# A graph layer's edge stage: the second layer two groups behind the first, and eight buffers for gathered rows

## The chip, the cores and the metric

The kernel runs on one core of one Trainium2 chip. The metric is the device time of an execution in microseconds. TensorE is called PE here, VectorE DVE, ScalarE ACT, GpSimd POOL and SyncE SP.

## What is computed

Two layers of a graph network over 6250 nodes with 128 features and 100,000 edges, each with a residual and a normalisation. The first is attention over edges. The change is in the second, of which this is the core:

```
x = _layernorm(x + attention(x, ...))
row, col = src, dst
edge_in = concatenate([x[row], x[col], edge_features])
h = silu(edge_in @ eW1 + eb1)
edge_feat = silu(h @ eW2 + eb2)
agg = segment_sum(edge_feat, row, num_segments=6250)
out = silu(concatenate([x, agg]) @ nW1 + nb1) @ nW2 + nb2
x = _layernorm(x + out)
```

## The kernel before

The edges are sorted by source into 832 tiles of 128 edges, so that each tile's sources lie in one window of 128 nodes. The kernel has the stages count, place, score, softmax, weigh, middle, edges, node layers and normalisation, one after the other. The edge stage (`edges`, from L1670) takes the tiles in 208 groups of four, G = 4. All of a group's steps have their own function, and each engine runs its own loop over the groups (`each_group`): `step(g, r)` calls the works of that engine, each for the group at some distance `by` from g. The distances and the order of that list are the schedule; engines meet by semaphores alone. Some groups at both ends are written out, the rest is a hardware loop over RING = 4 groups.

Per group:

- SP loads rows of lane numbers for two groups at once, 256 KB (L1712), into one of two buffers.
- DVE `index` (L1733) turns the destinations into int32 for the gather. `front` makes the one-hot matrices of the sources (`ed_oht`, L1738) and copies the attributes (`ed_attrs`, L1742). `by_edges` makes one-hots the other way (`ed_ohf`, L1748). `back` adds the four sums to the table `vals` (L1758).
- POOL `gather` (L1724) issues four indirect DMAs, one a tile, each fetching 128 rows of 512 bytes by destination into `ed_bg`, a ring of four buffers. Before a gather it waits until the inputs of the group four earlier are done (`s_z`).
- PE `turn` (L1819) transposes the attributes into the one PSUM tile `ps_ed_oht`; `inputs` (L1829, L1831, L1834) makes a tile's first layer in `ps_z` (two PSUM banks): attributes, three bf16 parts of the source's row by one-hot, and the gathered row, transposed; `second` (L1842, L1845) is the second layer in `ps_ed_o` (two banks); `sums` (L1855) sums the features by source in `ps_ed_s` (two banks).
- ACT `turned` (L1791) copies the transposed attributes to SBUF (`ed_attr_t`, two buffers), `hidden` (L1796) makes `ed_hts` = silu of the first layer (two buffers), `feature` (L1801) makes `ed_efs` = silu of the second.

In an execution of `step(g)` PE does the transpose of g+1, the inputs of g, the sums of g-2 and the second layer of g-1, in that order. The sums of g-2 need ACT's `ed_efs` of g-2, whose second layer is the last thing of PE's step before. ACT does turned g+1, hidden g, feature g-1; DVE index g+3, front g+2, by_edges g, back g-3.

Of the kernel before, what the change touches and what calls it, by code (L numbers as in the profile page):

```python
# [651 lines left out]
RING = 4  # L652


def each_group(eng, step, lead=0, lag=0, groups=NG, rings=1):


    for g in range(-lead, rings * RING):
        step(g, g % RING)
    with eng.Fori(rings, groups // RING - 1) as i:  # L660
        for r in range(RING):
            step(RING * i + r, r)
    for g in range(groups - RING, groups + lag):
        step(g, g % RING)


def group_at(g, r, by, groups=NG):

    there = not isinstance(g, int) or 0 <= g + by < groups
    return g + by, (r + by) % RING, there  # L670


def ring_count(g, r, each):

    return (g - r + RING) * (each // RING)
# [993 lines left out]
def edges(c, a):  # L1669
# [7 lines left out]
    s_b = semaphores(nc, c.stack, "ed_b_in0 ed_b_in1 ed_b_in2 ed_b_in3")  # L1677
# [3 lines left out]
    with ExitStack() as t:  # L1681
# [4 lines left out]
        w2 = sb("w_2", [P, F], F32)  # L1686
# [4 lines left out]
        ohf = sb("ed_ohf", [P, RING, G, P], F32)  # L1691
# [11 lines left out]
        with nc.Block() as block:  # L1703
            @block.sync
            def _(sp):
                sp.dma_start(w2[:, :], a["eW2"]).then_inc(s_w, 16)
                sp.dma_start(b2[:, :], row_vector(a["eb2"], F)).then_inc(s_w, 16)

                def lanes(g, r):
                    if r % 2 == 0:  # L1710
                        wait_count(sp, s_oht, g - 2)
                        sp.dma_start(lane_rows[:, r // 2, :], lanes_of(c, g * G, 2 * G)).then_inc(s_lr[r // 2], 16)  # L1712
                each_group(sp, lanes, rings=2)

            @block.gpsimd
            def _(pool):
                pool.memset(attr[:, :, :], 0.0).then_inc(s_pad, 1)

                def gather(g, r):
                    pool.wait_ge(s_idx, g + 1)  # L1720
                    wait_count(pool, s_z, g - RING + 1)
                    pool.sem_inc(s_turn, 1)
                    for k in range(G):
                        pool.indirect_dma_start(bg[:, r, k * F:(k + 1) * F], None, c.b_dram[:, :],  # L1724
                                                bass.IndirectOffsetOnAxis(ap=idx[:, r, k:k + 1], axis=0)
                                                ).then_inc(s_b[r], 16)
                each_group(pool, gather)

            @block.vector
            def _(dve):  # L1730
                def index(g, r):
                    wait_count(dve, s_b[r], (g - r) * (16 * G // RING))
                    dve.tensor_copy(idx[:, r, :], c.rec[:, bass.ds(g * G, G), C_DST]).then_inc(s_idx, 1)  # L1733

                def front(g, r):
                    dve.wait_ge(s_lr[r // 2], ring_count(g, r, 16))
                    wait_count(dve, s_z, g - RING + 1)
                    dve.tensor_scalar(oht[:, r].rearrange("p k n -> p (k n)"),  # L1738
                                      lane_rows[:, r // 2, r % 2 * GP:(r % 2 + 1) * GP], c.pid[:, 0:1], None,
                                      ALU.is_equal).then_inc(s_oht, 1)  # L1740
                    wait_count(dve, s_tr, g - RING + 1)
                    dve.tensor_copy(attr[:, r, 0:K].rearrange("p (j x) -> p j x", j=3),  # L1742
# [3 lines left out]
                def by_edges(g, r):  # L1746
                    wait_count(dve, s_sum, g - RING + 1)
                    dve.tensor_tensor(ohf[:, r], c.iota[:, :].unsqueeze(1).to_broadcast([P, G, P]),  # L1748
# [11 lines left out]
                def step(g, r):  # L1760
                    for by, work in ((3, index), (2, front), (0, by_edges), (-3, back)):
                        at, slot, there = group_at(g, r, by)
# [21 lines left out]
                each_group(dve, step, lead=3, lag=3, rings=2)  # L1784

            @block.scalar
            def _(act):
                def turned(g, r):
                    act.wait_ge(s_tr, g + 1)
                    wait_count(act, s_z, g - 1)  # L1790
                    act.activation(att[:, r % 2, :], pst[:, 0:P], ACT.Copy).then_inc(s_att, 1)  # L1791

                def hidden(g, r):
                    act.wait_ge(s_z, g + 1)
                    wait_count(act, s_o, g - 1)
                    act.activation(ht[:, r % 2, :], psz[r % 2][:, :], ACT.Silu).then_inc(s_h, 1)  # L1796
# [7 lines left out]
                def step(g, r):  # L1804
                    for by, work in ((1, turned), (0, hidden), (-1, feature)):
                        at, slot, there = group_at(g, r, by)
                        if there:
                            work(at, slot)
                each_group(act, step, lead=1, lag=1, rings=2)

            @block.tensor
            def _(pe):
# [3 lines left out]
                def turn(g, r):  # L1816
                    pe.wait_ge(s_at, g + 1)
                    wait_count(pe, s_att, g)
                    pe.transpose(pst[:, 0:P], attr[:, r, :], c.identb[:, :]).then_inc(s_tr, 1)  # L1819

                def inputs(g, r):
# [5 lines left out]
                    for k in range(G):  # L1827
                        z = psz[b][:, k * P:(k + 1) * P]
                        pe.matmul(z, wc[:, k, :], att[:, b, :], start=True, stop=False)  # L1829
                        for j in range(3):  # L1830
                            pe.matmul(z, c.tab[:, j, bass.ds(win[k] * F, F)], oht[:, r, k, :], start=False, stop=False)  # L1831
                        if k == 0:
                            pe.wait_ge(s_b[r], ring_count(g, r, 16 * G))
# [4 lines left out]
                def second(g, r):  # L1838
# [5 lines left out]
                    for k in range(G):  # L1844
                        ins = pe.matmul(pso[b][:, k * F:(k + 1) * F], ht[:, b, k * P:(k + 1) * P], w2[:, :],  # L1845
# [3 lines left out]
                def sums(g, r):  # L1849
# [4 lines left out]
                    for k in range(G):  # L1854
                        ins = pe.matmul(pss[b][:, k * P:(k + 1) * P], ef[:, b, k, :], ohf[:, r, k, :],  # L1855
# [3 lines left out]
                def step(g, r):  # L1859
                    for by, work in ((1, turn), (0, inputs), (-2, sums), (-1, second)):  # L1860
                        at, slot, there = group_at(g, r, by)
# [172 lines left out]
```

## Time and profile before

| | us |
|---|---|
| median of 3 runs | 6032.9 |
| runs | 6025.1 to 6042.95 |
| profiled execution | 6037.5 |
| its span | 6035.8 |
| edge stage in it | 4577.6 to 5943.5 |
| POOL busy in the span | 3887.0 (64%) |
| PE busy in the span | 2949.4 (49%) |

The profile is of one execution; its own time stands 4.6 us over the median. Times in it count from the span's start. "Idle before" in a row is the time for which that engine did nothing before it, and the name behind it is what ended it: "issue" is nothing that the profile shows, "remote" a semaphore whose sender it can't name. The end of a matmul is modelled, its start is recorded. A name such as `ps_z<-ident,ed_bg` reads output, arrow, inputs; buffer numbers are left out.

### The profile page before, as it was taken

How to read it: one execution, taken by the hardware profiler on the slowest of the kernel's cores; microseconds unless marked ns; L12 is line 12 of the kernel's file. 1: busy time of each engine (PE TensorE's matmuls, PEld its weight loads, DVE VectorE, ACT ScalarE, POOL GpSimd, SP SyncE). 2: the span in 40 equal slices, each digit the busy share in tenths (PEclk: the TensorE clock that was granted, in tenths of full speed). 3: DMA queues.
4: the chain of work that ended last, by engine and by line, in shares of the span. 5: the costliest groups of instructions: out<-in, count | busy, mean ns of one | idle time of the engine just before them, and what ended most of it. 6: DMA issues, size and time to landing. Idle time of an engine off the chain costs nothing. (4 is left out here: it accounts for less than half of the span.)

```text
span 6035.8 us, 82769 instructions
## 1 busy us (share of the span) xinstructions
PE 2949.4 (49%) x21843; PEld 2592.4 (43%) x21844; DVE 2376.2 (39%) x6253; ACT 765.7 (13%) x1646; POOL 3887.0 (64%) x4130
## 2 busy tenths in 40 slices
PE   6444443442222222212666666566474666666666
PEld 4333332331222222212555555555454565565554
DVE  6554555552222222348333333333253333333334
ACT  0111110110000000001111111111121221122112
POOL 0677887885666666641888888888814555555551
PEclk9765565665566666556777788877766888888888
DMA  2200000002222222210443434343351222222222
GB/s 90 87 10 10 11 11 11 11 11 90 66 66 66 67 65 64 67 41 8 35 36 35 36 35 36 35 36 35 35 145 53 59 61 60 62 60 60 60 60 60
DMA packets 299979, 293.29 MB, mean 49 GB/s; under 512 B 61763, under 2 KB 239104, under 8 KB 298911
## 3 DMA queue, kind: packets, MB, share of 16 engines
q0 software_dynamic: 200128, 176.61, 18.5%
q1 hardware_dynamic: 96926, 103.02, 6.0%
q10 hardware_dynamic: 2880, 13.11, 0.5%
q8 instruction: 21, 0.34, 0.0%
q14 instruction: 24, 0.20, 0.0%
HBM read 198.61 MB, written 93.92 MB: 48 GB/s over the span
## 5 line engine op out<-in xcount | busy, mean ns | idle before, releaser
L1080 POOL DMA_INDIRECT sums_dram<-we_merged_rows,we_idx x832 | 1286.2, 1546 | 420.4 <-issue 206.7
L1724 POOL DMA_INDIRECT ed_bg<-b_rows_dram,ed_idx x832 | 796.4, 957 | 563.1 <-issue 284.9
L787 POOL DMA_INDIRECT sc_k<-k_rows_dram,sc_idx x832 | 797.0, 958 | 441.3 <-issue 253.8
L642 POOL DMA_INDIRECT records_dram<-rec_out,row_idx x784 | 783.0, 999 | 207.3 <-issue 111.0
L873 PE MATMUL ps_q<-tab,sc_oht 128*128 x1664 | 307.6, 360 | 825.9 <-DVE sc_oht L802 414.2
L873 PEld LDWEIGHTS ps_q<-tab,sc_oht 128*128 128x128 f32 x1664 | 288.1, 269 | 842.0 <-issue 842.0
L1231 PE MATMUL ps_merged<-we_rows,we_same_dst 128*128 128x129 f32 x1664 | 332.0, 361 | 586.5 <-issue 438.0
L1758 DVE TENSOR_TENSOR vals<-vals,ps_ed_s 128x128 f32 x832 | 239.0, 287 | 848.4 <-PE ps_ed_s L1855 403.8
L1231 PEld LDWEIGHTS ps_merged<-we_rows,we_same_dst 128*128 128x128 f32 x1664 | 283.4, 257 | 622.2 <-issue 612.8
L817 DVE TENSOR_TENSOR sc_prods<-ps_q,sc_k 128x1024 f32<-128x1024 f32 x104 | 127.2, 1223 | 821.8 <-remote 756.5
L1855 PE MATMUL ps_ed_s<-ed_ohf,ed_efs 128*128 128x128 f32 x1664 | 281.1, 322 | 337.3 <-ACT ed_efs L1801 291.7
L1133 DVE SCALAR_TENSOR_TENSOR we_firsts<-we_merged_rows,lane_unmark,two_marks 128x4 f32<-128x4 f32 x208 | 46.3, 222 | 1013.5 <-ACT we_merged_rows L1176 1013.5
L1855 PEld LDWEIGHTS ps_ed_s<-ed_ohf,ed_efs 128*128 128x128 f32 x1664 | 247.1, 228 | 362.3 <-issue 337.6
L593 PE MATMUL ps_table<-place_ohw,place_oh 128*128 128x400 bf16 (+7 forms) x784 | 160.9, 381 | 450.0 <-DVE place_ohw L216 337.0
L1831 PE MATMUL ps_z<-ed_oht,tab 128*128 128x128 bf16 x2496 | 309.1, 228 | 63.1 <-issue 62.3
L593 PEld LDWEIGHTS ps_table<-place_ohw,place_oh 128*128 128x128 bf16 x784 | 111.3, 162 | 508.9 <-issue 452.3
L1211 PE MATMUL ps_dst_row<-ident,we_dsts 128*128 128x128 f32 x1664 | 329.7, 366 | 0.0
L1211 PEld LDWEIGHTS ps_dst_row<-ident,we_dsts 128*128 128x128 f32 x1664 | 314.6, 281 | 0.0
L629 POOL COPY rec_out<-records 128x16 f32 (+1 forms) x784 | 190.7, 252 | 183.2 <-POOLq L276 112.1
L1176 ACT ACTIVATE we_merged_rows<-ps_merged 128x516 f32<-128x516 f32 x208 | 124.8, 600 | 1280.0 <-DMA sums_dram<-we_merged_rows,we_idx 1265.9
L1221 PE MATMUL ps_v<-value_tab,we_oht 128*128 x1664 | 276.0, 318 | 0.1
L1845 PEld LDWEIGHTS ps_ed_o<-w,ed_hts 128*128 128x128 f32 x1664 | 262.2, 224 | 18.4 <-issue 4.3
(291 smaller groups left out, 6230.3 us busy)
## 6 DMA issues: line engine op xcount, KB each, us to landing
sc_lane_rows<-lanes_dram SPq DMA_DIRECT2D x104, 256.0 KB
ed_lane_rows<-lanes_dram SPq DMA_DIRECT2D x104, 256.0 KB
sc_k<-k_rows_dram,sc_idx POOLq DMA_INDIRECT x832
sums_dram<-we_merged_rows,we_idx POOLq DMA_INDIRECT x832
ed_bg<-b_rows_dram,ed_idx POOLq DMA_INDIRECT x832
sums_dram<-zero_rows ACTq DMA_DIRECT2D x20, 640.0 KB, 10.2
records_dram<-rec_out,row_idx POOLq DMA_INDIRECT x784
mi_rows<-sums_dram SPq DMA_DIRECT2D x48, 256.0 KB, 4.4
```

The lines of the kernel that those rows point to most:

```text
L593: ins = pe.matmul(table[:, k:PG, :], ohl[:, b, :, k], ohw[:, b, k, :].unsqueeze(1).to_broadcast([P, PG - k, WC]), start=(k == 0), stop=Tru ...
L642: pool.indirect_dma_start(c.rec_rows, bass.IndirectOffsetOnAxis(ap=idx[:, b, j:j + 1], axis=0), out[:, b, j, :], None, bounds_check=SLOTS ...
L787: pool.indirect_dma_start(kg[:, r, k * F:(k + 1) * F], None, c.k_dram[:, :], bass.IndirectOffsetOnAxis(ap=idx[:, r, k:k + 1], axis=0)).the ...
L873: ins = pe.matmul(psq[b][:, k * F:(k + 1) * F], oht[:, b, k, :], c.qtab[:, bass.ds(win[k] * F, F)], start=True, stop=True)
L1080: pool.indirect_dma_start(c.acc_dram[k][:, :], bass.IndirectOffsetOnAxis(ap=idx[:, r, k:k + 1], axis=0), rows[:, r, k, 0:F], None, compute ...
L1211: ins = pe.matmul(psd[:, k * P:(k + 1) * P], dst[:, r, k:k + 1].to_broadcast([P, P]), c.ident[:, :], start=True, stop=True)
L1221: ins = pe.matmul(psv[b][:, k * F:(k + 1) * F], oht[:, b, k, :], c.vtab[:, bass.ds(win[k] * F, F)], start=True, stop=True)
L1231: ins = pe.matmul(merged[b][:, k, 0:F + 1], same[:, b, k, :], con[:, b, k, :], start=True, stop=True)
L1724: pool.indirect_dma_start(bg[:, r, k * F:(k + 1) * F], None, c.b_dram[:, :], bass.IndirectOffsetOnAxis(ap=idx[:, r, k:k + 1], axis=0)).the ...
L1831: pe.matmul(z, c.tab[:, j, bass.ds(win[k] * F, F)], oht[:, r, k, :], start=False, stop=False)
L1845: ins = pe.matmul(pso[b][:, k * F:(k + 1) * F], ht[:, b, k * P:(k + 1) * P], w2[:, :], start=False, stop=(k == G - 1))
L1855: ins = pe.matmul(pss[b][:, k * P:(k + 1) * P], ef[:, b, k, :], ohf[:, r, k, :], start=True, stop=True)
```

## The change

All of it is in the edge stage. Its loops run over eight groups instead of four, on all engines. Distances change as in the table.

| engine | before | after |
|---|---|---|
| PE | turn +1, inputs 0, sums -2, second -1 | turn +2, inputs 0, second -2, sums -3 |
| ACT | turned +1, hidden 0, feature -1 | turned +2, hidden 0, feature -2 |
| DVE | index +3, front +2, by_edges 0, back -3 | index +7, front +3, by_edges -1, back -4 |

`ed_bg` and `ed_idx` have eight buffers instead of four, `ed_attr_t` and `ed_hts` four instead of two. PSUM stays as it was. To make room, `ed_ohf`, `ed_efs` and the weights `w_2` move into free columns of the table `work`, and carry that name in the rows of order below.

```
@@ edges, buffers
+        w2 = c.work[:, NP - F:NP]
+        spare = lambda n, m: c.work[:, NT * 3 + n * GP:NT * 3 + m * GP].rearrange("p (b k n) -> p b k n", b=m - n, k=G)
+        ohf = spare(0, RING)
-        att = sb("ed_attr_t", [P, 2, P], BF16)
-        idx = sb("ed_idx", [P, RING, G], I32)
-        bg = sb("ed_bg", [P, RING, G * F], F32)
+        att = sb("ed_attr_t", [P, RING, P], BF16)
+        idx = sb("ed_idx", [P, ER, G], I32)
+        bg = sb("ed_bg", [P, ER, G * F], F32)
-        ht = sb("ed_hts", [P, 2, GP], F32)
-        ef = sb("ed_efs", [P, 2, G, F], F32)
+        ht = sb("ed_hts", [P, RING, GP], F32)
+        ef = spare(RING, RING + 2)
@@ gpsimd, gather
-                    wait_count(pool, s_z, g - RING + 1)
+                    wait_count(pool, s_z, g - ER + 1)
@@ scalar
-                    wait_count(act, s_z, g - 1)
+                    wait_count(act, s_z, g - RING + 1)
...
-                    wait_count(act, s_o, g - 1)
+                    wait_count(act, s_o, g - RING + 1)
@@ tensor, step
-                    for by, work in ((1, turn), (0, inputs), (-2, sums), (-1, second)):
-                        at, slot, there = group_at(g, r, by)
+                    for by, work in ((2, turn), (0, inputs), (-2, second), (-3, sums)):
+                        at, slot, there = group_at(g, r, by, NG, ER)
...
-                each_group(pe, step, lead=1, lag=2, rings=2)
+                each_group(pe, step, lead=2, lag=3, ring=ER)
```

On PE, inside the loop, this stands in a row before, from the last matmul of a group's inputs to the first of the next (ISA and REGISTER_ALU are register work of the sequencer):

```order
L1834 MATMUL ps_z1<-ident,ed_bg 128x128
L88 ISA
L1855 MATMUL ps_ed_s1<-ed_ohf,ed_efs 128x128 x4
L1842 MATMUL ps_ed_o0<-b_2_rows,ones 128x512
L1845 MATMUL ps_ed_o0<-w_2,ed_hts 128x128 x4
L1819 MATMUL ps_ed_oht<-identb,ed_attrs 128x128
```

And at the same place after:

```order
L1837 MATMUL ps_z1<-ident,ed_bg 128x128
L1845 MATMUL ps_ed_o1<-b_2_rows,ones 128x512
L1848 MATMUL ps_ed_o1<-work,ed_hts 128x128 x4
L88 ISA
L1858 MATMUL ps_ed_s0<-work 128x128 x4
L1820 REGISTER_ALU
L1822 MATMUL ps_ed_oht<-identb,ed_attrs 128x128
```

The second layer has moved ahead of the sums and is of the group two back, the sums of the group three back.

On DVE, at the opening of the stage, before:

```order
L1782 SCALAR_TENSOR_TENSOR b_2_rows<-b_2_parts,ident,b_2_rows 128x128 x2
L1733 CAST ed_idx<-records 128x4 x2
L1738 TENSOR_SCALAR ed_oht<-ed_lane_rows,partition_number 128x512
L1742 COPY ed_attrs<-work 128x72
L1733 CAST ed_idx<-records 128x4
```

And after:

```order
L1785 SCALAR_TENSOR_TENSOR b_2_rows<-b_2_parts,ident,b_2_rows 128x128 x2
L1736 CAST ed_idx<-records 128x4 x5
L1741 TENSOR_SCALAR ed_oht<-ed_lane_rows,partition_number 128x512
L1745 COPY ed_attrs<-work 128x72
L1736 CAST ed_idx<-records 128x4
```

Five groups of gather indices stand ahead of the first one-hot instead of two.

## Rows read from the trace of the kernel before

**Rows 1.** Busy time by stretch: the score stage, the edge stage.
```profile
core 0: us, PE busy (x) PEld busy (x) DVE busy (x) ACT busy (x) POOL busy (x), PEclk, DMA share, GB/s
1428.00:2672.00 1244.00, 329.32 (x1768) 301.55 (x1768) 357.39 (x622) 35.52 (x154) 797.01 (x832) 0.61 0.26 66
4577.60:5943.50 1365.90, 901.64 (x7904) 819.75 (x7903) 477.24 (x1658) 272.87 (x625) 796.41 (x832) 0.82 0.24 60
```

**Rows 2.** Group of the gathers: busy, mean ns, idle before and what ended it.
```profile
L1724 POOL DMA_INDIRECT ed_bg<-b_rows_dram,ed_idx x832 | 796.4, 957 | 563.1 <-issue 284.9 <-remote 165.5 <-PE ps_z L1834 88.8
```

**Rows 3.** Timeline, the edge stage's end: start, us, instruction, idle before.
```profile
5926.79 0.94 POOL L1724 DMA_INDIRECT ed_bg<-b_rows_dram,ed_idx  x1 [0.30 <-issue]
...
5932.84 1.05 PE L1845 MATMUL ps_ed_o<-w,ed_hts 128*128 128x128 f32 x8
...
5936.20 1.05 PE L1845 MATMUL ps_ed_o<-w,ed_hts 128*128 128x128 f32 x8
```

**Rows 4.** Waits of the edge stage: total us, times, longest us.
```profile
ACT ed_efs L1801 <- remote: 496.9, 53, 10.7
...
PE ps_ed_s L1855 <- ACT ed_efs L1801: 291.7, 56, 8.3
...
PE ps_z L1834 <- DMA ed_bg<-b_rows_dram,ed_idx: 6.7, 2, 4.6
```

**Rows 5.** Timeline of one cycle of four groups in the edge stage.
```profile
5035.04 0.60 ACT L1796 ACTIVATE ed_hts<-ps_z 128x512 f32<-128x512 f32 x1 [4.85 <-remote]
...
5035.78 0.94 POOL L1724 DMA_INDIRECT ed_bg<-b_rows_dram,ed_idx  x1 [1.83 <-issue]
...
5037.47 1.05 PE L1845 MATMUL ps_ed_o<-w,ed_hts 128*128 128x128 f32 x8
...
5039.66 0.28 PE L1834 MATMUL ps_z<-ident,ed_bg 128*128 128x128 f32 x1
...
5044.52 0.94 POOL L1724 DMA_INDIRECT ed_bg<-b_rows_dram,ed_idx  x1 [0.30 <-issue]
5047.35 0.60 ACT L1801 ACTIVATE ed_efs<-ps_ed_o 128x512 f32<-128x512 f32 x1 [10.56 <-remote]
...
5048.08 2.07 PE L1855 MATMUL ps_ed_s<-ed_ohf,ed_efs 128*128 128x128 f32 x8 [8.14 <-ACT ed_efs L1801]
5048.25 0.94 POOL L1724 DMA_INDIRECT ed_bg<-b_rows_dram,ed_idx  x1 [2.79 <-remote]
...
5049.94 0.63 PE L1842 MATMUL ps_ed_o<-b_rows,ones 128*128 128x512 bf16 x1
...
5050.37 1.92 PE L1845 MATMUL ps_ed_o<-w,ed_hts 128*128 128x128 f32 x8
...
5054.93 0.94 POOL L1724 DMA_INDIRECT ed_bg<-b_rows_dram,ed_idx  x1 [1.99 <-PE ps_z L1834]
```

**Rows 6.** Busy time by stretch: that cycle, and after its late signal.
```profile
5026.00:5052.00 26.00, 16.48 (x152) 15.23 (x150) 9.43 (x35) 5.13 (x12) 15.20 (x17) 0.81 0.23 61
...
5047.50:5054.00 6.50, 5.92 (x41) 5.68 (x42) 2.21 (x8) 1.87 (x5) 3.78 (x4) 0.61 0.16 44
```

**Rows 7.** Timeline of the edge stage's opening.
```profile
4591.02 0.42 PE L1834 MATMUL ps_z<-ident,ed_bg 128*128 128x128 f32 x1
...
4601.44 0.94 POOL L1724 DMA_INDIRECT ed_bg<-b_rows_dram,ed_idx  x1 [0.30 <-issue]
...
4606.03 0.60 ACT L1796 ACTIVATE ed_hts<-ps_z 128x512 f32<-128x512 f32 x1 [12.49 <-remote]
```

**Rows 8.** DMA queues of 4700 to 5900: packets, MB, share of 16 engines.
```profile
q0 software_dynamic: 23522, 48.22, 16.1%
q1 hardware_dynamic: 13251, 24.13, 7.8%
```

**Rows 9.** Waits of the score stage.
```profile
DVE sc_prods L817 <- remote: 756.5, 47, 28.7
```

More of the change, by code:

```diff
@@ L652, with each_group, group_at, ring_count @@
 RING = 4
[L655 to L667, printed above, removed]
+SR = 8
+ER = 8
+def each_group(eng, step, lead=0, lag=0, groups=NG, rings=1, ring=RING):
+    for g in range(-lead, rings * ring):
+        step(g, g % ring)
+    with eng.Fori(rings, groups // ring - 1) as i:
+        for r in range(ring):
+            step(ring * i + r, r)
+    for g in range(groups - ring, groups + lag):
+        step(g, g % ring)
+def group_at(g, r, by, groups=NG, ring=RING):
     there = not isinstance(g, int) or 0 <= g + by < groups
-    return g + by, (r + by) % RING, there
-def ring_count(g, r, each):
-    return (g - r + RING) * (each // RING)
+    return g + by, (r + by) % ring, there
+def ring_count(g, r, each, ring=RING):
+    return (g - r + ring) * each // ring
 def load_windows(eng, c, regs, side, g, n=1):
@@ L1676, in edges @@
     s_lr = semaphores(nc, c.sems, "ed_lanes_in0 ed_lanes_in1")
-    s_b = semaphores(nc, c.stack, "ed_b_in0 ed_b_in1 ed_b_in2 ed_b_in3")
+    s_b = semaphores(nc, c.stack, " ".join(f"ed_b_in{n}" for n in range(ER)))
     (s_turn,) = semaphores(nc, c.sems, "ed_gather_turn")
@@ L1726, in gather @@
                                                 ).then_inc(s_b[r], 16)
-                each_group(pool, gather)
+                each_group(pool, gather, ring=ER)
             @block.vector
@@ L1760, in step @@
                 def step(g, r):
-                    for by, work in ((3, index), (2, front), (0, by_edges), (-3, back)):
-                        at, slot, there = group_at(g, r, by)
+                    for by, work in ((7, index), (3, front), (-1, by_edges), (-4, back)):
+                        at, slot, there = group_at(g, r, by, NG, ER)
                         if there:
@@ L1783, in _ @@
                                              in1=b2k[:, :], op0=ALU.mult, op1=ALU.add).then_inc(s_bias, 1)
-                each_group(dve, step, lead=3, lag=3, rings=2)
+                each_group(dve, step, lead=7, lag=4, ring=ER)
             @block.scalar
@@ L1804, in step @@
                 def step(g, r):
-                    for by, work in ((1, turned), (0, hidden), (-1, feature)):
-                        at, slot, there = group_at(g, r, by)
+                    for by, work in ((2, turned), (0, hidden), (-2, feature)):
+                        at, slot, there = group_at(g, r, by, NG, ER)
                         if there:
                             work(at, slot)
-                each_group(act, step, lead=1, lag=1, rings=2)
+                each_group(act, step, lead=2, lag=2, ring=ER)
             @block.tensor
```

36 lines of the change are left out of this document (17 added, 19 removed).

## The prediction, made before the changed kernel ran

> **What bounds the kernel now.** The change touches only the edge stage, so I first cut the trace into stages: 1365.9 of the 6035.8 us are the edge stage, from the first gather to the last addition [rows 1]. There PE is busy for 902 us, POOL for 796 us, DVE and ACT far less. No engine fills the stage; it is bound by a chain. A gather instruction takes 957 ns on average [rows 2] with 0.30 us to the next [rows 3], 1.25 us in all, and there are 832: POOL alone would need 832 × 1.25 = 1040 us. PE alone, at the end of the stage where nothing stops it, starts the second layer of one group at 5932.84 and of the next at 5936.20 [rows 3], 3.4 us a group, 707 us for 208 groups. The stage runs at 1350 us from the first gather at 4577.6 to the end of the last at 5927.7 [rows 3], 6.49 us a group.
>
> The waits of the stage say who stands still [rows 2, 4]: PE before the sums for 291.7 us, all on the activation of the features (L1801); ACT before that activation for 496.9 us, on something the profile can't name ("remote"); POOL for 165.5 and 88.8 us on freed gather buffers. PE waits on landed gathers (L1834) for 6.7 us in all. So gathered rows are always there in time, and POOL's pauses come from PE.
>
> The timeline of one cycle shows what "remote" is [rows 5]. PE's last matmul of a second layer starts in the row at 5037.47 and that row ends at 5038.5; the next inputs end at 5039.9. ACT, idle for 10.56 us, starts the features only at 5047.35. Its one unmet condition is that second layer: the end of a matmul is known to the others 8.8 us after the record says it was over. POOL, too, waits for the end of the inputs recorded at 5039.9 and resumes at 5048.25. PE has meanwhile reached the sums and stands for 8.14 us. I call this a late signal. The late signals come out together about 2 us after POOL has run out of gathers (its last one before ends at 5045.5). Such a cycle takes 26.0 us and four groups [rows 6]; a weaker one is at its start, where ACT gets an ended input layer after 4.85 us idle, at 5035.04 [rows 5].
>
> The Trainium skill ("Perfetto Trace Analysis", the section on per-engine timelines) says that the end shown for TensorE is estimated and that the semaphore follows once PSUM has acknowledged the writes. This trace agrees that the two can differ, here by 8.8 us; the page gives no reason for such a size, and nothing below uses it.
>
> **The change part by part.** No matmul, activation, addition or transfer is added or removed; 832 gathers and 104 loads of lane rows stay.
>
> *Order on PE.* Before: transpose, inputs of g, sums of g-2, second layer of g-1. After: transpose of g+2, inputs of g, second layer of g-2, sums of g-3. Between the end of a second layer and the sums that need it there was one input layer, after it an input layer, another second layer and the transpose. With prompt signals neither order holds PE up: the groups of [rows 3] follow each other at 3.4 us. Under a late signal PE now gets further. At 5039.9 it has the inputs done and stands at the sums, which are 2.07 us when done at 5048.08 and are followed by a second layer of 0.63 + 1.92 us, at a granted clock of 0.61 [rows 5, 6], the lower level (1.2 GHz) for most of it. These 4.2 us stand between the release at 5047.3 and the next input layer. In the new order they depend on older signals and would lie before the stop; after the release PE goes straight to the input layer. That layer's end permits POOL's next gather. It came at about 5054, and POOL paused 1.99 us before 5054.93 [rows 5]; 4.2 us earlier is 49.8, before POOL is through with the gathers it has (5053.0). The pause shrinks to the usual 0.30: 1.69 us a cycle. I take exactly this, because POOL at 1.25 us a gather then is the later of the two. The other two pauses of the cycle, 2.79 and 1.83 us [rows 5], stay: they end with a late signal, which the order doesn't touch. 1350 us / 26.0 = 52 cycles, 52 × 1.69 = **-88 us**. Bounds: zero, if PE stops at another step just as early; and 52 × (1.69 + 2.49 + 1.53) = -297 us if all three pauses go.
>
> *What could stop PE instead.* The transposed attributes have one PSUM tile, so the transpose of g+3 waits for ACT's copy of g+2, whose transpose is one step old. That is one whole step (3.4 us) against the 1.5 us of an input layer before. PE therefore still stops inside every late signal, one step later at most: this is why I don't take more than one pause.
>
> *ACT and DVE.* ACT's order stays turn, hidden, feature with the feature two behind; nothing is queued behind a new wait that was not there. DVE's one-hots (L1738) for g+3 now wait for the inputs of g-1 instead of g-2 before g+2; behind that wait stand the additions of g-4, and PE's transpose waits for DVE. DVE needs 0.35 + 0.18 us to produce them; a whole PE step lies between. Zero while that holds; if a late signal catches it, PE stops where it would have stopped anyway.
>
> *Eight buffers of gathered rows.* In the cycle they hide nothing, since PE waits for landed rows for 6.7 us in the whole stage [rows 4]. They change the ends of the stage. At the opening, POOL ran five groups without a stop, until the gather of 4601.44; ACT's signal from PE's second input layer, recorded as over by 4591.4, came at 4606.03 [rows 7]. With eight buffers POOL may run nine groups. If signals come only when it stops, that is 4 × 5.0 = **+20 us**; the lower bound is zero. At the close POOL is up to four more groups ahead, and those run at 3.4 instead of 6.49 us: 4 × 3.1 = **-12 us**.
>
> *Loops of eight groups.* Half as many branches, twice the code. In the steady part of the stage there are no instruction transfers: the queues between 4700 and 5900 are two, both of data [rows 8]. The Trainium skill ("Runtime: NRT & Kernel Launch", instruction fetch mechanics) warns that a taken branch to code outside the resident pages forces a fetch. This trace shows no such fetch for a loop of four groups, and can't show one for eight. I take zero. As a bound from rows: 24 returns of the loop, each at worst a pause like the 2.79 us one, is +67 us.
>
> **Sum.** -88 + 20 - 12 = -80 us on the profiled execution's 6037.5 us, 5957.5. That execution is 4.6 us over the median of the runs; against the median, 6032.9 - 80 = **5953 us**.
>
> **The rivals.**
> *Nothing to gain (chance 0.17).* The late signals set the pace alone, whatever the order. For: ACT's 496.9 us of "remote" are longer than PE's 291.7. Against: the 4.2 us of work that stood after the release. Then the opening's +20 and the close's -12 remain, 6041 us.
>
> *The deep ring frees POOL (0.16).* In the score stage the ring holds 32 tiles too (4 buffers of 8), and its 832 gathers took 1244 us with the same late signals (DVE waits for "remote" 756.5 us there) [rows 1, 9]. At that pace the edge stage's 1366 us shrink by 122, 5911 us. If the late signals lost their grip entirely, the stage would be POOL's 1040 us and some 16 us of close, 310 less, 5723 us; I give this end 0.07 of the 0.16.
>
> *The deep ring feeds the late signals (0.21).* They come out when POOL stops. With room for eight groups POOL can run longer before it stops, and PE stands meanwhile, as at the opening, where a signal was 14.6 us late during a run of five groups. Where a cycle's longest run grows by one group it costs 5.0 us. Against: in a steady state POOL can only refill what PE has freed, two groups a run, whatever the depth. It decides from the point where PE, running at 3.4 us against POOL's 5.0, leaves POOL a backlog of more than two groups when a late signal begins. At one group more in every second cycle, with no pause saved: 26 × 5.0 = +130, 6163 us; in every cycle 6293 us.
>
> *The change doesn't do what it says.* The order on PE shows that it does; no chance of its own.
>
> **How the numbers follow.** One pause of three saved has 0.46, the largest share: 5953 us, in itself 5925 to 6000. With 0.16 for the deep ring, 0.17 for nothing and 0.21 for longer late signals the shares are complete. What a measurement of this kernel can tell from no change is about 0.3%, 18 us. Faster by more than that: 0.46 + 0.16 = 0.62; within it 0.17; slower 0.21. The range for 8 in 10 goes down to 5850 (two pauses of three gone, 52 × (1.69 + 1.53) = 167 us, and some), leaving out the 0.07 of a freed POOL, and up to 6080, leaving out some 0.12 of longer late signals.
>
> **What would show it.** In the profile after: PE's wait before the sums (291.7 us) nearly gone, with one before the transpose or the inputs in its place that is smaller; POOL's idle time before the gathers (563.1 us, of which 250 are the 0.30s) down to about 480; a cycle of about 24.3 us for four groups. The edge stage at 1286 us. ACT still waits for "remote" in pieces of 5 to 9 us. If these pieces are 14 us and more, and POOL runs more than two groups between pauses, the third rival is right. If PE's idle time merely moves and POOL's pauses stay three a cycle, the first is. Instruction transfers between 4700 and 5900 would mean that the longer loop costs. The forecast is wrong in its root if late signals have nothing to do with POOL's stops, since then the eight buffers and the saved pause are priced on the wrong row.

## The result and the profile after

The changed kernel takes 6069.2 us (median of 6, 6061.0 to 6102.0), the kernel before on the same chip 6028.7 us (median of 6). The ratio is 1.0072, with a 95% interval of 1.0058 to 1.0086: slower, where the forecast was 5953 us. The profiled execution took 6066.8 us.

Everything ahead of the edge stage is 7 us shorter (it starts at 4571.0 instead of 4577.6), and what stands behind it is as long as before. The edge stage goes from 1366 to 1402.7 us. Its row, from the first gather to the last addition (columns as in [rows 1]):

```profile
4571.00:5973.70 1402.70, 1035.33 (x7904) 902.31 (x7903) 482.55 (x1656) 286.90 (x625) 831.51 (x832) 0.79 0.24 58
```

The gathers' group (busy, mean ns, idle before and what ended it; [rows 2] is its answer before) and DVE's additions, from the profile after:

```profile
L1727 POOL DMA_INDIRECT ed_bg<-b_rows_dram,ed_idx x832 | 831.5, 999 | 550.0 <-issue 238.7 <-DVE ed_idx L1736 190.3 <-remote 110.8
L1761 DVE TENSOR_TENSOR vals<-vals,ps_ed_s 128x128 f32 x832 | 238.9, 287 | 581.2 <-remote 439.7
```

The additions in the kernel before, in the grouping of its edge stage:

```profile
L1758 DVE TENSOR_TENSOR vals<-vals,ps_ed_s 128x128 f32 x832 | 239.0, 287 | 848.4 <-PE ps_ed_s L1855 403.8 <-remote 341.5 <-issue 13.6
```

Before, POOL waited for the index like this (total us, times, longest):

```profile
POOL ed_bg L1724 <- DVE ed_idx L1733: 23.8, 23, 9.4
```

And waits after ([rows 4] before):

```profile
POOL ed_bg L1727 <- DVE ed_idx L1736: 190.3, 69, 9.4
DVE ed_oht L1741 <- remote: 292.3, 76, 36.8
ACT ed_hts L1799 <- remote: 403.0, 78, 35.5
ACT work L1804 <- remote: 277.6, 60, 8.7
DVE vals L1761 <- remote: 439.7, 85, 10.4
PE ps_ed_s L1858 <- issue: 103.7, 167, 1.2
```

Two things are new. PE's 291.7 us before the sums are gone, as forecast: no row for ACT stands there now, but "issue" pieces of 103.7 us do. And POOL, which waited for freed buffers, now waits for DVE's conversion of the indices (`ed_idx`), 190.3 us in 69 waits. The 69 are not alike: one of 9.4 us is the stage's first gather, which waits as long in the kernel before; 27 are the 0.30 us that stand between any two gathers; the other 41 take 4.2 us on average, 173 us in all. One such place in the timeline after (start, us, instruction, idle before):

```profile
5009.60 1.06 PE L1858 MATMUL ps_ed_s<-work 128*128 128x128 f32 x8
...
5015.20 0.95 POOL L1727 DMA_INDIRECT ed_bg<-b_rows_dram,ed_idx  x1 [0.30 <-issue]
...
5018.08 1.57 DVE L1761 TENSOR_TENSOR vals<-vals,ps_ed_s 128x128 f32 x4 [7.75 <-remote]
...
5018.10 0.60 ACT L1799 ACTIVATE ed_hts<-ps_z 128x512 f32<-128x512 f32 x1
...
5019.57 0.16 DVE L1736 CAST ed_idx<-records 128x4 int32 x1
...
5020.60 1.01 POOL L1727 DMA_INDIRECT ed_bg<-b_rows_dram,ed_idx  x1 [4.45 <-DVE ed_idx L1736]
```

Late signals arrive together at 5018.1: ACT gets its input layer, and DVE the sums, whose row on PE starts at 5009.60 and ends 7.4 us before. POOL ran out at 5016.15. But DVE's next work is the additions for g-4 (1.57 us), and only behind them stands the index for g+7. POOL resumes at 5020.60, 2.5 us later than the signal and 0.87 us after the index is made. In [rows 5] it resumed 0.90 us after ACT on a late signal; so some 1.6 of the 2.5 us are DVE's.

It is the additions that hold the index up. Ahead of each of the 41 waits, DVE's last long wait was the one before the additions, on "remote", and not the one before the one-hots. In the kernel before, in the cycle of [rows 5], the additions had started on time, and the index was made 7.5 us ahead of the late signal:

```profile
5038.17 1.58 DVE L1758 TENSOR_TENSOR vals<-vals,ps_ed_s 128x128 f32 x4
5039.67 0.16 DVE L1733 CAST ed_idx<-records 128x4 int32 x1
```

There PE stood in front of the next sums, and those of the older group had been signalled: 403.8 us of DVE's wait before the additions end directly on PE's sums, 341.5 us on "remote". Now PE goes on through second layer and sums, and a larger part of the sums' signals is late: 439.7 of 581.2 us are on "remote". This reading of the two rows of additions fits the places looked at; what the place of the index is worth is tested below.

### The profile page after: what moved, and what is told of

It is laid out like the page before. It is cut to its first block and busy times, and to the rows that moved or that the text cites. A ratio compares the mean times of both kernels' runs of the same rounds, so it can differ in the third digit from the quotient of the medians.

```text
span 6065.1 us, 82347 instructions
## 1 busy us (share of the span) xinstructions
PE 3093.8 (51%) x21843; PEld 2678.6 (44%) x21844; DVE 2383.3 (39%) x6253; ACT 780.3 (13%) x1646; POOL 3927.4 (65%) x4130
## 5 line engine op out<-in xcount | busy, mean ns | idle before, releaser
L1082 POOL DMA_INDIRECT sums_dram<-we_merged_rows,we_idx x832 | 1287.0, 1547 | 420.5 <-issue 208.9
L1727 POOL DMA_INDIRECT ed_bg<-b_rows_dram,ed_idx x832 | 831.5, 999 | 550.0 <-issue 238.7
L875 PE MATMUL ps_q<-tab,sc_oht 128*128 x1664 | 311.8, 364 | 796.4 <-DVE sc_oht L804 436.6
L1761 DVE TENSOR_TENSOR vals<-vals,ps_ed_s 128x128 f32 x832 | 238.9, 287 | 581.2 <-remote 439.7
L1834 PE MATMUL ps_z<-ed_oht,tab 128*128 128x128 bf16 x2496 | 349.8, 253 | 96.2 <-issue 95.3
L1858 PE MATMUL ps_ed_s<-work 128*128 128x128 f32 x1664 | 300.4, 316 | 104.8 <-issue 103.7
L1848 PE MATMUL ps_ed_o<-work,ed_hts 128*128 128x128 f32 x1664 | 302.1, 323 | 62.2 <-issue 59.0
L1848 PEld LDWEIGHTS ps_ed_o<-work,ed_hts 128*128 128x128 f32 x1664 | 284.9, 235 | 106.1 <-issue 92.0
L1858 PEld LDWEIGHTS ps_ed_s<-work 128*128 128x128 f32 x1664 | 260.9, 227 | 117.8 <-issue 116.7
L1837 PE MATMUL ps_z<-ident,ed_bg 128*128 128x128 f32 x832 | 276.6, 332 | 35.8 <-issue 30.2
```

Of the source, the lines that this page charges most:

```text
L875: ins = pe.matmul(psq[b][:, k * F:(k + 1) * F], oht[:, b, k, :], c.qtab[:, bass.ds(win[k] * F, F)], start=True, stop=True)
L1082: pool.indirect_dma_start(c.acc_dram[k][:, :], bass.IndirectOffsetOnAxis(ap=idx[:, r, k:k + 1], axis=0), rows[:, r, k, 0:F], None, compute ...
L1834: pe.matmul(z, c.tab[:, j, bass.ds(win[k] * F, F)], oht[:, r % RING, k, :], start=False, stop=False)
L1837: ins = pe.matmul(z, bg[:, r, k * F:(k + 1) * F], c.ident[:, :], start=False, stop=True, is_transpose=True)
L1848: ins = pe.matmul(pso[b][:, k * F:(k + 1) * F], ht[:, r % RING, k * P:(k + 1) * P], w2[:, :], start=False, stop=(k == G - 1))
```

## Experiments

A ratio is always to the kernel before, run in between on the same chip. The kernel before took 6029, 5964 and 5965 us on three chips, and 5516, 5521 and 5521 us on three others. What that is comes under "the chip"; until then all runs are on the slower three, but for the paced ones. Where two kernels ran on different chips, compare their ratios and not their times.

### The two halves apart

`order_alone` has four buffers and loops of four in the changed kernel:

```
-ER = 8
+ER = 4
...
-                    for by, work in ((7, index), (3, front), (-1, by_edges), (-4, back)):
+                    for by, work in ((3, index), (3, front), (-1, by_edges), (-4, back)):
```

> The new order (second layer two groups behind, sums three, additions four, one-hots three ahead) with four buffers of gathered rows and loops of four groups, so without the other half of the change. Theory 1, the index queued behind the one-hots: in the profile after the change POOL waits 69 times, 190.3 us in all, 2.76 us each, for DVE's index, because DVE now stands before the one-hots of g+3 until the inputs of g-1 are known to be done, and behind that wait stand 0.5 us of one-hots, 0.7 us of the one-hot by edges and 1.6 us of additions before the next index. This order has the same slack of one group, so by theory 1 it is as slow as the whole change, 6060 to 6080 us, with POOL waiting for ed_idx again. Theory 2, the deep ring feeds the late signals: the order alone keeps its gain, 5950 us. Theory 3, the loop of eight groups costs: about 6030 us, as before.

Measured: 6072.9 us, ratio 1.0063 (1.0044 to 1.0081). Here, too, POOL waits for the index in 50 places inside the stage, each behind DVE's wait before the additions. The group of gathers in its profile:

```profile
L1727 POOL DMA_INDIRECT ed_bg<-b_rows_dram,ed_idx x832 | 822.6, 989 | 584.5 <-issue 244.2 <-DVE ed_idx L1736 234.8 <-remote 93.3
```

`ring_alone` keeps the eight buffers and puts back all of the old order:

```
-                    for by, work in ((7, index), (3, front), (-1, by_edges), (-4, back)):
+                    for by, work in ((7, index), (2, front), (0, by_edges), (-3, back)):
...
-                    for by, work in ((2, turn), (0, inputs), (-2, second), (-3, sums)):
+                    for by, work in ((1, turn), (0, inputs), (-2, sums), (-1, second)):
```

> The old order with eight buffers of gathered rows, index seven ahead and loops of eight groups. Theory 1 (index queued): the one-hots are two ahead and the index stays two groups ahead of what POOL needs, so POOL does not wait for it; 6030 us, perhaps some 20 more for a longer opening. Theory 2 (deep ring feeds the late signals): slower by the third rival's price, 6100 us or more, with POOL running more than two groups between pauses. Theory 3 (long loop): 6060 us or more, PE's idle pieces called issue at the place where the loop returns.

Measured: 6034.6 us, ratio 1.0010 (1.0000 to 1.0020).

```profile
L1727 POOL DMA_INDIRECT ed_bg<-b_rows_dram,ed_idx x832 | 803.7, 966 | 540.5 <-issue 244.0 <-remote 192.6 <-PE ps_z L1837 80.2
```

The loss is the order's, and the wait for the index comes with the order. Eight buffers, an index seven ahead and loops of eight together cost 6 us (12 at the interval's upper end). The third rival's price (130 us) and that of a longer loop fall.

### The index out of the way

`index_early` is the changed kernel with one line of DVE's order changed (and the lead from 7 to 8):

```
-                    for by, work in ((7, index), (3, front), (-1, by_edges), (-4, back)):
+                    for by, work in ((3, front), (8, index), (-1, by_edges), (-4, back)):
```

> The changed kernel with DVE's index for g+8 right behind the one-hots for g+3, ahead of the one-hot by edges and the additions, instead of the index for g+7 behind all of them. Nothing else moves. Theory 1: POOL's 190.3 us of waiting for the index go, 69 x 2.76; what of it the freed buffers or late signals do not take back is the gain, 5960 to 6010 us. Theory 2 and theory 3: unchanged, 6069 us, with POOL waiting for PE or for remote events where it waited for the index.

`ahead_four` gives the index a lead of four more groups in another way, by holding POOL back:

```
-                    wait_count(pool, s_z, g - ER + 1)
+                    wait_count(pool, s_z, g - RING + 1)
```

> The changed kernel, in which POOL may gather only four groups ahead instead of eight (it waits for the inputs of g-4 instead of g-8); buffers, order, index and loops of eight are those of the change. Theory 1: the index is now made seven ahead and needed three ahead, so POOL never waits for it; 5960 to 6000 us. Theory 2: as fast as the order alone, 5950 us. Theory 3: no better than the change, 6070 us. Theories 1 and 2 are told apart by the order alone.

Measured: `index_early` 6013.0 us, 0.9972 (0.9962 to 0.9983); `ahead_four` 6005.6 us, 0.9959 (0.9947 to 0.9971), each some 3 to 6 us above what theory 1 allowed. The gathers of `index_early`, then of `ahead_four`:

```profile
L1727 POOL DMA_INDIRECT ed_bg<-b_rows_dram,ed_idx x832 | 844.4, 1015 | 476.7 <-issue 252.7 <-remote 202.2 <-PE ps_z L1837 12.4
```

```profile
L1727 POOL DMA_INDIRECT ed_bg<-b_rows_dram,ed_idx x832 | 843.7, 1014 | 481.0 <-issue 379.9 <-remote 77.5 <-DVE ed_idx L1736 15.8
```

The place of one 0.16-us instruction in DVE's queue is worth 56 us: more than the whole loss. With it out of the way the change is faster than the kernel before, by 16 us (by 23 where POOL stays four ahead). In `index_early` the one-hots for g+3, with their new wait, still stand in front of the index; only the one-hot by edges and the additions have gone behind it. So it was these that cost, not the one-hots' wait.

`order_early_third` needs nothing of the eight buffers: `order_alone` with the index for g+4 behind the one-hots for g+3.

```
-                    for by, work in ((3, index), (3, front), (-1, by_edges), (-4, back)):
+                    for by, work in ((3, front), (4, index), (-1, by_edges), (-4, back)):
```

> order_index_early, unchanged, on another chip. Where signals are late (before 5960 us or more), theory 1, that the index in DVE's queue was the order's whole loss: ratio 0.995 to 0.998. Theory 2, that the eight buffers or the loops of eight are needed: 1.000 to 1.006. Where they are prompt (before some 5520 us): 0.998 a third time.

Measured: 5941.9 us against 5964.7, ratio 0.9959 (0.9945 to 0.9972). Theory 1 holds: the index was the order's whole loss, and eight buffers and longer loops are not needed. This and `ahead_four` are the best versions found.

```profile
L1727 POOL DMA_INDIRECT ed_bg<-b_rows_dram,ed_idx x832 | 838.1, 1007 | 474.2 <-issue 253.8 <-remote 203.3 <-DVE ed_idx L1736 9.4
```

### Where the rest of the expected 88 us is

POOL's idle time falls in `ahead_four` from 563.1 [rows 2] to 481.0 us, 82 less, almost the 88 forecast. But the gathers themselves are busy for 843.7 instead of 796.4 us, 47 more, and the close grows by 4: -82 + 47 + 4 = -31 us, the measured change of the stage (1366.2 to 1335.2). The longer gathers are these, in the profile of the change:

```profile
5044.19 0.68 DVE L1751 TENSOR_TENSOR work<-iota,lanes 128x512 f32<-128x512 f32 x1
...
5044.23 1.47 POOL L1727 DMA_INDIRECT ed_bg<-b_rows_dram,ed_idx  x1 [0.30 <-issue]
...
5046.00 0.95 POOL L1727 DMA_INDIRECT ed_bg<-b_rows_dram,ed_idx  x1 [0.30 <-issue]
```

A gather that starts while the by-edges one-hot runs takes until some 0.8 us after the one-hot's end. Over the trace, the 75 gathers that start within 0.3 us behind a one-hot's start take 1.25 to 1.46 us (means of each tenth); those that start ahead of it take about 0.95. All 132 gathers over 1.1 us overlap this one-hot (23 in the kernel before). The additions, which read PSUM, lengthen none by themselves (203 gathers overlap them alone, 0.957 us at most). The Trainium skill ("GPSIMD Engine Reference", key points) says that GpSimd shares its SBUF interfaces with VectorE, with contention from VectorE instructions that have two SBUF inputs; this instruction has two, and the traces agree. With the new order far more gathers meet a one-hot (166 of over 1.1 us in `ahead_four`); probably because one signal now releases DVE and POOL together.

To see what that costs, three kernels hold the one-hot's row of numbers (`iota`) in a spare bank of PSUM (`psi`), on top of `ahead_four`, of the kernel before, and of `index_early`:

```
+                dve.tensor_copy(psi[:, 0:P], c.iota[:, :]).then_inc(s_pad, 1)
...
-                    dve.tensor_tensor(ohf[:, r % RING], c.iota[:, :].unsqueeze(1).to_broadcast([P, G, P]),
+                    dve.tensor_tensor(ohf[:, r % RING], psi[:, 0:P].unsqueeze(1).to_broadcast([P, G, P]),
```

> The changed kernel with POOL four groups ahead (as ahead_four), and the row of numbers that the by-edges one-hot (L1751) compares with held in PSUM instead of SBUF, so that the one-hot reads one operand from PSUM like the additions do. Theory 1, the one-hot holds up the start of a gather: in the changed kernel all 132 gathers over 1.1 us overlap this one-hot, and those that start within its last 0.4 us take 1.25 to 1.46 us instead of 0.945; in ahead_four they are 166 with 54 us of excess. With the operand in PSUM they go, the mean gather is back at 945 to 960 ns, and the kernel gains most of the 54 us over ahead_four's 6005.6: 5955 to 5975 us. Theory 2, the long gathers are a symptom (they fall after a late signal, when everything starts at once) and not a cost of the one-hot: unchanged, 6005 us, the long gathers stay. Theory 3: they go, but POOL only waits longer for PE instead: 6000 us with POOL's idle time up by the 54 us.

> The kernel before with the same one edit (the by-edges one-hot's row of numbers in PSUM). Its trace has 23 gathers over 1.1 us with 8.7 us of excess. Theory 1: a gain of at most 9 us, 6020 us, about what can be measured. Theory 2 and 3: 6029 us. If the edit by itself made the one-hot slower or faster on DVE it would show here too; DVE is not on the path, so that should cost nothing.

> The changed kernel with all eight groups ahead, the index right behind the one-hots (as index_early) and the row of numbers in PSUM. Theory 1: index_early's 6013.0 less most of its 58 us of excess: 5960 to 5980 us. Theory 2 and 3: 6005 to 6013 us.

Measured: 0.9973 (0.9963 to 0.9983), 1.0006 (0.9997 to 1.0015) and 0.9996 (0.9987 to 1.0005). The gathers of `four_iota_psum`, then of `before_iota_psum`:

```profile
L1728 POOL DMA_INDIRECT ed_bg<-b_rows_dram,ed_idx x832 | 784.9, 943 | 527.7 <-issue 401.9 <-remote 102.0 <-DVE ed_idx L1737 18.9
```

```profile
L1725 POOL DMA_INDIRECT ed_bg<-b_rows_dram,ed_idx x832 | 787.4, 946 | 549.4 <-issue 300.0 <-remote 143.9 <-PE ps_z L1836 89.7
```

The long gathers are gone (mean 943 ns), and nothing is gained: theory 3. `early_iota_psum` is worse than expected: it has lost all of `index_early`'s gain (0.9996 against 0.9972). `order_early_psum`, the same edit on `order_early_third` and on the same chip, shows it side by side: busy 838.1 to 787.8, idle 474.2 to 532.0, ratio 0.9978 (0.9969 to 0.9987) against 0.9959, 9 us slower.

> The new order, four buffers, loops of four, the index for g+4 right behind the one-hots for g+3, and the by-edges one-hot's row of numbers in PSUM. Where signals are prompt POOL is never idle beyond its 0.30 us between gathers, so each long gather costs its full excess: order_index_early has 8 to 12 us of it, the kernel before 16, so 10 us less than order_index_early, a ratio of 0.9960 to 0.9972. Where signals are late: as order_index_early, since POOL's pauses take the time back.

```profile
L1728 POOL DMA_INDIRECT ed_bg<-b_rows_dram,ed_idx x832 | 787.8, 947 | 532.0 <-issue 304.3 <-remote 174.5 <-PE ps_z L1839 43.5
```

So where signals are late, time taken out of POOL's gathers comes back as pauses. Where no gather is lengthened, the new order saves 549.4 - 527.7 = 22 us of pauses, not 82: the rest had only moved from idle to busy. The count of the pauses longer than 0.6 us says the same. The kernel before has 152 (the forecast's 3 times 52 is 156), `ahead_four` 116; with the numbers in PSUM the old order has 152 and the new one 139. On the old order the edit is neutral (1.0006), and the one-hot takes as long from PSUM (689 ns against 691). Why it costs all three kernels of the new order 0.14 to 0.24% is open.

### What makes the signals late

`no_lane_loads` is the kernel before without 102 of the 104 loads of lane rows that SP issues beside POOL; it reads the first two pieces again and again, so the one-hots of the sources are those of other edges, and its output is not the layer's.

```
-                each_group(sp, lanes, rings=2)
+                for g in (0, 2):
+                    lanes(g, g)
...
-                    dve.wait_ge(s_lr[r // 2], ring_count(g, r, 16))
+                    dve.wait_ge(s_lr[r // 2], 16)
```

> The kernel before, whose edge stage loads only the first two of its 104 pieces of lane rows (256 KB each) and then reads the same two again and again; the destinations' one-hots are thus those of other edges. This asks what makes PE's signals late. In the stage of the weighed sums POOL sends as steadily and no engine issues other transfers, and there no signal is late; in the three stages where SP loads beside POOL they are. Theory A, SP's loads are the other half of the cause: the late signals go, PE's matmuls run at their undisturbed 3.4 us a group and the edge stage falls from 1366 us to POOL's own pace, 1060 to 1150 us, some 5720 to 5810 us in all. Theory B, POOL's gathers alone delay PE's signals: edge stage 1366 us, 6029 us in all. In between, if fewer of them come: the rest has another cause.

Measured: ratio 0.9989 (0.9980 to 0.9998), and the edge stage still waits as before:

```profile
ACT ed_efs L1803 <- remote: 458.5, 61, 10.3
```

SP's loads are not the cause: without nearly all of them the lateness stays, and the kernel gains 7 us. POOL's pace was to be the next suspect, with a memset behind every gather (128 x 64 here, 128 x 440 in `pace_large`):

```
+                        pool.wait_ge(s_turn, 9 * g + 1 + 2 * k)
+                        pool.sem_inc(s_turn, 1)
+                        pool.memset(c.work[:, NP - 64:NP], 0.0).then_inc(s_turn, 1)
```

> The kernel before with a memset of 128 x 64 f32 on POOL behind each gather of the edge stage (one in a spare part of the work buffer, nothing reads it), about 0.25 us, so that gathers leave every 1.5 us instead of 1.25. In the stage of the weighed sums POOL's instruction takes 1547 ns and one leaves every 1.85 us; no signal of PE is late there. Theory B1, signals are late when gathers leave faster than they land: with room between them the signals are prompt, and the edge stage is POOL's own 832 x 1.5 = 1250 us and some 20: 5925 to 5950 us on a chip where before takes 6029. Theory B2, signals are late while POOL is busy and come when it pauses: each of the 832 memsets makes POOL's runs longer, and the stage grows by most of 832 x 0.25 = 208 us, 6180 to 6240. Theory B3, nothing about POOL's pace matters and the pauses absorb it: 6030 to 6060.

> As pace_small with a memset of 128 x 440 f32, about 0.55 us, so that a gather leaves every 1.85 us as in the stage of the weighed sums. Theory B1: prompt signals whatever pace_small shows, edge stage 832 x 1.85 = 1540 us, and no pause of POOL beyond. Theory B2: late signals as before with pauses of 2 to 3 us that come as often: 1366 + 832 x 0.6 = 1870 us, 6530 in all. Theory B3: PE's matmuls keep the pace, the stage is at POOL's 1540 us or a little over with late signals still in it.

> pace_small, unchanged (a memset of 128 x 64 f32 behind each gather), on the chip of this call. Measured where no signal is late: POOL waits 149 us for the memset's semaphore in all and a gather leaves every 1.31 us, ratio 1.0037. With late signals: theory B1 (signals are late when gathers leave faster than they land) 0.93 to 0.99 with lateness down; theory B2 (late while POOL is busy, whatever it does) 1.005 to 1.03; theory B3 (POOL's pace plays no part, its pauses absorb the memsets) 0.999 to 1.003.

> pace_small, unchanged (a memset of 128 x 64 f32 behind each gather; where signals are prompt a gather leaves every 1.31 us with it instead of 1.27, ratio 1.0038), on another chip. If its signals are late (before 5960 us or more): theory B1, signals are late when gathers leave faster than they land: 0.93 to 0.99 with lateness down. Theory B2, they are late while POOL is busy and come only when it stops: 1.005 to 1.03, as many pauses as before. Theory B3, POOL's pace plays no part and its pauses absorb the memsets: 0.999 to 1.003. If its signals are prompt, it repeats 1.0038.

All paced runs fell on chips where no signal is late, so they don't answer it, and none of the theories B1 to B3 is tested. There the small memset costs 1.0037, 1.0038 and 1.0046 (intervals of 0.0012 to 0.0017 to either side), the large one 1.0511 (1.0495 to 1.0527): its gathers leave every 1.61 us, not the 1.85 expected, and fill the stage, 1352 us. Whether POOL's pace makes the signals late stays open.

### The chip

`order_index_early` is the kernel of `order_early_third`; on its chip the kernel before took 5516 us, 512 less than where the forecast was made. So the kernel before and the change were looked at again on such a chip.

> The new order with four buffers of gathered rows and loops of four (as order_alone), and DVE's index for g+4 right behind the one-hots for g+3. No part of the eight buffers is left. Theory 1, the index in the queue was the order's whole loss and the eight buffers only widen the opening: as good as ahead_four or index_early, a ratio to the kernel before of 0.995 to 0.998, with POOL waiting 0 to 20 us for the index instead of order_alone's 234.8. Theory 2, eight buffers or loops of eight are needed for ahead_four's gain (0.9959): a ratio of 1.000 to 1.006.

> The kernel before, unchanged, profiled on the chip of this call. Three chips gave 6029, 5964 and 5516 us for it. Theory C, late signals are the chip's: where it takes some 5516 us, ACT never waits for remote events, PE's signals come at once and the edge stage is POOL's own 832 x 1.25 + 15 = 1060 us; where it takes 5960 us or more, the edge stage is 1340 to 1366 us with 8 us of lateness in every cycle of four groups. Nothing in between.

> The change, unchanged, on the chip of this call. Without late signals POOL's gathers fill the stage, and by theory 1 DVE's index is in time when PE's signals are (a step of PE is 3.4 us, one group of gathers 5.0 us), so the ratio is within 0.997 to 1.000. With late signals: 1.006 to 1.008 as before.

> order_index_early, unchanged (new order, four buffers, loops of four, index for g+4 right behind the one-hots for g+3), on the chip of this call. With late signals, theory 1 (the index in DVE's queue was the whole loss): ratio 0.995 to 0.998, POOL's wait for the index 0 to 20 us. Theory 2 (eight buffers or loops of eight are needed): 1.000 to 1.006. Without late signals: 0.998 as measured there.

`before_again` took 5524.5 us. Its edge stage, its gathers, and two waits:

```profile
4356.50:5430.30 1073.80, 820.61 (x7904) 734.89 (x7903) 491.36 (x1658) 284.95 (x625) 807.78 (x832) 0.98 0.31 76
```

```profile
L1724 POOL DMA_INDIRECT ed_bg<-b_rows_dram,ed_idx x832 | 807.8, 971 | 262.8 <-issue 247.6 <-DVE ed_idx L1733 13.0 <-PE ps_z L1834 2.1
```

```profile
ACT ed_hts L1796 <- PE ps_z L1834: 452.5, 207, 6.5
PE ps_z L1834 <- DMA ed_bg<-b_rows_dram,ed_idx: 248.7, 181, 4.6
```

There is no late signal: ACT's waits end on PE by name, 207 of 208 times, POOL has no idle time but the 0.30 us between gathers (262.8 us), and the stage is POOL's, 1073.7 us, 18 more than the prediction reckoned for a freed POOL (1040 and 16). It is the same program. All times of the kernel before fall into one group or the other, 5510 to 5534 us or 5956 to 6043, as theory C has it. Whether it is the chip or a state that lasted through a set of runs, these runs can't tell.

On such chips the change is 1.0005 (0.9996 to 1.0014), no change: DVE's index is in time when PE's signals are (9.7 us of waiting in its profile, 9.4 of them at the stage's first gather). The new order with the early index is 0.9978 (0.9968 to 0.9988) and, as `order_early_again`, 0.9981 (0.9972 to 0.9990). There a lengthened gather does cost its full excess: `order_early_again` has 799.9 us busy against the change's 807.3 on that chip, and a stage of 1067.1 against 1074.6.

```profile
L1727 POOL DMA_INDIRECT ed_bg<-b_rows_dram,ed_idx x832 | 799.9, 961 | 262.8 <-issue 240.6 <-DVE ed_idx L1736 18.2 <-PE ps_z L1837 4.0
```

## Why the prediction was wrong

- **What bounds the stage: right** for the chip of the forecast. POOL's pauses end with PE's signals, late ones above all, and PE's stop before the sums was real; it went from 291.7 us to nothing.
- **ACT and DVE, "Zero while that holds": the step that failed.** The term saw the additions of g-4 only as work behind the one-hots' new wait, and asked only who waits for the one-hots. It left out POOL, which waits for the index, and the wait that the additions have themselves. The index stands behind the additions; they wait for PE's sums; and in the new order a larger part of the sums' signals is late. The sentence "if a late signal catches it, PE stops where it would have stopped anyway" took this as harmless. But POOL is not PE: it then waits until DVE has added, some 1.6 us more each time. What the runs showed in place of zero: 173 us of waiting for the index in 41 places, and 56 us of the kernel's time (the change against `index_early`), which turns the gain of 16 us into a loss of 40.
- **The order's gain, 52 x 1.69 = 88 us: the direction is right, the size is not.** This term failed too, with less weight. Idle time fell by 82 us in `ahead_four`, nearly what was forecast, but the stage by 31, and by 22 in pauses where no gather is lengthened. The term took POOL's pause as the thing saved, and PE as 4.2 us further on when the signals come. But of PE's 291.7 us before the sums, some 190 came back in the change as "issue" pieces between PE's own instructions (last section): where PE had stood still it now moves slowly, and gets less far than reckoned. `order_early_psum` shows the other half: 50 us taken out of POOL's gathers came back as 58 us of pauses. What sets the length of the cycle stays open.
- **The opening, +20, and the close, -12: right, together and singly.** `ring_alone` is +6 us against the forecast's +8. Counted from the first gather, in one trace of each kernel, ACT starts on the 21st group's input layer at 172.3 us instead of 151.7, 21 us later: the opening. That lag is 11 us at the 200th group and 2 us at the last: 9 us come back in the last eight groups, the close, and 10 on the way, which the forecast did not have. POOL's first stop comes after nine groups, and ACT's wait there is 32.7 us (35.5 in the change), against 12.5 [rows 7].
- **Loops of eight, zero: right.** `ring_alone` has them and costs 6 us in all. In the change one instruction transfer falls between 4700 and 5900 where there was none [rows 8]:

```profile
q8 instruction: 1, 0.02, 0.0%
```

- **Third rival (0.21), the right sign by the wrong mechanism.** POOL's long run comes at the opening only; the longest late waits elsewhere are 8.7 us for ACT's features and 10.4 for DVE's additions, and `ring_alone`, which has the deep ring, does not lose what the rival priced (130 us). So the 0.21 that the forecast gave to slower is met by luck, by a mechanism it did not have; and 6069 us lies inside the range of 5850 to 6080 for the same reason. First rival, nothing to gain (6041 us): without the index this would have been nearer than the forecast's 5953, at 6005 to 6013.
- **The root.** The forecast was said to be wrong at its root if late signals have nothing to do with POOL's stops. That is not settled, since no paced kernel ran where signals are late. What the runs do show: on three of six chips there are no late signals at all, and a cycle of 26 us read from one trace belonged to that chip or its state.

## What to carry to other kernels

When a step moves, find every wait whose signal moves with it, on other engines too. List everything that stands behind such a wait, small conversions for another engine's DMA above all, and count the lead that each consumer keeps. A lead counted in groups is worth what lies between the two signals; where signals come together it is worth little, so put the conversion of a DMA's index ahead of waits and long work that it does not need. And before a pause is priced as a saving, ask what sets the length of the whole cycle: a pause that shrinks while its neighbour grows has saved nothing.

## What the runs showed of the hardware

The same program takes 5516 to 5521 us on three chips and 5964 to 6029 us on three others. Between `before_again` (5523 us) and the kernel before at the forecast (6036 us) the difference is in three of the four stages with indirect transfers of POOL. From the first transfer to the last the place stage is 1165 us there and 1210 here, the score stage 1053 and 1237, the edge stage 1061 and 1350. The fourth, the stage of the weighed sums, with scatters of 1547 ns, is 1540 us on both. The granted clock of the edge stage is 0.98 there and 0.82 here, with PE idle more here.

Where signals are late, PE's own rows are odd too. At the opening of the kernel before and of the change PE itself starts one instruction every 1.4 to 2.8 us while it waits for nothing that the profile shows, and POOL gathers without a stop. In the change:

```profile
4601.41 0.26 PE L1834 MATMUL ps_z<-ed_oht,tab 128*128 128x128 bf16 x1 [2.54 <-issue]
...
4604.21 0.26 PE L1834 MATMUL ps_z<-ed_oht,tab 128*128 128x128 bf16 x1 [2.54 <-issue]
```

This lasts until some 3 us after POOL runs out, at 4615.8. PE's "issue" pieces in the edge stage grew from some 160 to some 350 us with the change, while its wait on ACT (291.7 us) went. The records may be ahead of what PE has really finished; no run here shows that, and what slows PE on these chips is open.
